# The block-diagonal keys of layer 2: four scaled copies on ACT in place of one instruction on DVE

## The reference

```python
HD, GROUPS = 8, 4
q = hidden_state @ Wq + bq
k = encoder_hidden_state @ Wk + bk
v = encoder_hidden_state @ Wv + bv
q = q.reshape(b, l, KVH, GROUPS, HD).transpose(0, 2, 3, 1, 4)
k = k.reshape(b, s, KVH, HD).transpose(0, 2, 1, 3)
v = v.reshape(b, s, KVH, HD).transpose(0, 2, 1, 3)
scores = jnp.einsum('bkgld,bksd->bkgls', q, k) / sqrt(HD) + encoder_attention_mask
attn = jax.nn.softmax(scores, axis=-1)
out = jnp.einsum('bkgls,bksd->bkgld', attn, v) ... @ Wo + bo
x = out + hidden_state          # then layer norm with gamma and beta
```

## Time and profile before

| what | value |
|---|---|
| median of 3 runs | 1674.97 us (1672.3 to 1674.98) |
| the profiled execution: its own time, its span | 1674.09 us, 1672.4 us |
| mean granted TensorE clock | 0.969 |
| busy share of the span: PE, PEld, DVE, ACT, POOL | 92%, 79%, 66%, 40%, 27% |
| layer 2, from its first instruction to its last | 1188.9 to 1354.9 us of the span |

### The profile page before, as it was taken

One profiled execution on the slowest core, in us unless ns is written; L12 is line 12 of the kernel. 1 busy time (PEld: TensorE's weight loads), 2 busy tenths in 40 slices (PEclk: granted clock), 3 DMA queues, 4 the chain that ended last, 5 costly groups with the idle time before them and its releaser, 6 DMA issues. The chain is left out here.

```text
span 1672.4 us, 33255 instructions
## 1 busy us (share of the span) xinstructions
PE 1545.5 (92%) x13291; PEld 1321.8 (79%) x13291; DVE 1103.6 (66%) x2377; ACT 672.5 (40%) x1270; POOL 454.6 (27%) x533
## 2 busy tenths in 40 slices
PE   4988999999999999999999999799788869999797
PEld 2656888888888888888888888789667748887697
DVE  6886666666666776667666666555499945776443
ACT  4654433343433434333333334332366634454221
POOL 2004020020110221200201110232288866562110
PEclk9998999999999999999999999999899979999899
DMA  4000010010000000000100000000410000000001
GB/s 131 1 0 26 14 39 14 1 39 14 27 13 14 26 14 14 26 14 13 39 14 9 31 26 11 20 20 0 84 56 1 2 1 2 3 2 2 1 1 50
DMA packets 44466, 34.12 MB, mean 20 GB/s; under 512 B 10658, under 2 KB 41384, under 8 KB 44200
## 3 DMA queue, kind: packets, MB, share of 16 engines
q1 hardware_dynamic: 44328, 32.17, 6.7%
HBM read 30.00 MB, written 2.10 MB: 19 GB/s over the span
## 5 line engine op out<-in xcount | busy, mean ns | idle before, releaser
L964 DVE STREAM_TRANSPOSE att_pt<-att_prob 32x256 f32<-32x256 f32 x496 | 215.7, 435 | 6.4
L864 ACT ACTIVATE split_q_sb<-psum,g_cols 128x512 f32<-128x512 f32 x128 | 88.3, 690 | 321.7 <-PE psum L732 321.7
L781 PE MATMUL psum<-att_wo_hi,att_ot_hi 128*128 128x256 f32 x512 | 149.2, 291 | 2.5 <-DVE att_ot_lo L977 1.4
L935 DVE TENSOR_REDUCE att_rmax<-psum 128x6 f32<-128x390 f32 (+1 forms) x96 | 49.2, 513 | 151.3 <-PE psum L694 151.3
L781 PE MATMUL psum<-att_wo_lo,att_ot_hi 128*128 128x256 f32 x512 | 144.6, 282 | 0.0
L781 PE MATMUL psum<-att_wo_hi,att_ot_lo 128*128 128x256 f32 x512 | 144.6, 282 | 0.0
L764 PE MATMUL psum<-att_pt,att_v_sb 128*128 128x128 f32 x1024 | 128.6, 279 | 3.5 <-DVE att_ot_lo L977 3.5
L987 DVE TENSOR_TENSOR g_x_res<-psum,g_x_res 128x256 f32<-128x256 f32 x128 | 54.3, 424 | 114.7 <-PE psum L781 88.3
L764 PEld LDWEIGHTS psum<-att_pt,att_v_sb 128*128 128x128 f32 x1024 | 122.9, 193 | 7.9 <-DVE att_ot_lo L977 3.7
L867 ACT ACTIVATE att_k_sb<-psum,g_cols 128x512 f32<-128x512 f32 x128 | 88.1, 688 | 80.9 <-PE psum L732 80.9
L732 PE MATMUL psum<-split_feat_hi,split_wide_hi 128*128 128x512 f32 x256 | 103.7, 405 | 4.5 <-DVE split_feat_lo L1011 3.3
(11 more groups left out here) (287 smaller groups left out, 3944.8 us busy)
## 6 DMA issues: line engine op xcount, KB each, us to landing
g_ctx_f<-in_L_xattn_wq SPq DMA_DIRECT2D x32, 128.0 KB, 2.2
g_ctx_f<-in_L_xattn_wk SPq DMA_DIRECT2D x32, 128.0 KB, 2.3
g_ctx_f<-in_L_xattn_wv SPq DMA_DIRECT2D x8, 512.0 KB, 3.8
g_ctx_f<-in_L_xattn_wo SPq DMA_DIRECT2D x8, 512.0 KB, 3.8
c_ctx_tok<-in_ctx SPq DMA_DIRECT2D x4, 512.0 KB, 5.6
g_x_res<-in_x SPq DMA_DIRECT2D x4, 512.0 KB, 8.7
g_w<-in_L_xattn_mlp_w SPq DMA_DIRECT2D x2, 1024.0 KB
out<-g_x_res SPq DMA_DIRECT2D x1, 2048.0 KB, 7.5
```

The costliest lines, as they stand in the source:

```text
L781: mm = pe.matmul(o_ps[p % 2], a, b, start=(h == 0 and t == 0), stop=(not last and h == HG - 1 and t == 2))
L864: act.activation(q_sb[:, h, :], q_ps[:, :], ACT.Identity, bias=G.cols[:, layer, head:head + 1]).then_inc(q_ready, 1)
L935: dve.tensor_reduce(rmax[:, a:b], s_ps[group][:, :, :], X_AXIS, ALU.max).then_inc(max_done, 1)
L964: turned = dve.transpose(pt[to:to + 32, :, :, r, u, 32 * a:32 * a + 32].rearrange("p h a t -> p (h a) t"), by_pair[of:of + 32, :, u, 32 * ...
```

## The change

Three things are edited, all in `phase_grouped_attention`. `place_keys` is taken out of DVE's list, and `move_projected` on ACT gets four more activations between the queries and the values. Each writes one `k_bd[:, v, :]` (128x128) as Identity(scale * k_ps + bias), with a column of `spread` as scale and a column of the new tile `k_bias` as bias; the last one raises `k_done`. `k_bias` is made once, before the loop, by a DVE instruction on 128x4 that multiplies `spread` with the key bias, and ACT waits for it once. Last, `project(p)` on PE, which overwrites the PSUM bank, now waits for `v_done` in place of `k_done`, since the values are now the last that is read from the bank.

```diff
--- before.py
+++ after.py
@@ -1779,7 +1779,7 @@
         wq, wk = m.sb("wq", [P, KT, D]), m.sb("wk", [P, KT, P])
         cols, bv_wide, one = m.sb("cols", [P, 4]), m.sb("bv_wide", [P, P]), m.sb("one", [1, P])
         mask = m.sb("mask", [P, B, T])
-        folded, spread = m.sb("folded", [P, ROWS]), m.sb("spread", [P, 4])
+        folded, spread, k_bias = m.sb("folded", [P, ROWS]), m.sb("spread", [P, 4]), m.sb("k_bias", [P, 4])
         q_sb, k_bd = m.sb("q_sb", [P, 2, 2, 2, T]), m.sb("k_bd", [P, 2, 4, P])
         v_bd = m.sb("v_bd", [P, 4, 2, 2, 2 * ROWS])
         soft = m.sb("soft", [P, 2, TILES, 4, 2, T])
@@ -1793,6 +1793,7 @@
         c_ps, o_ps = c_bank[:, 0:D].rearrange("p (b c t) -> p b c t", b=2, c=2), c_bank[:, 0:D]
         cols_ps, bias_ps = p_bank[:, 0:4], c_bank[:, 0:D]
 
+        k_bias_done = m.sem("k_bias_done")
         mask_in, arrived, v_zero, folded_made, spread_made, one_made = (m.sem(n) for n in
             ("mask_in", "arrived", "v_zero", "folded_made", "spread_made", "one_made"))
         w_ready, cols_psum, cols_done, bv_done, bias_psum, bias_done = (m.sem(n) for n in
@@ -1859,7 +1860,7 @@
                 def project(p):
                     x_new, ctx = (t[:, :, p * P:(p + 1) * P] for t in (G.feat_f, G.ctx_f))
                     if p:
-                        pe.wait_ge(k_done, p)
+                        pe.wait_ge(v_done, p)
                     for c in range(2):
                         accumulate(q_ps[:, c, :], [(wq[:, k, c * P:(c + 1) * P], x_new[:, k, :]) for k in range(KT)])
                     accumulate(k_ps, [(wk[:, k, :], ctx[:, k, :]) for k in range(KT)])
@@ -1949,6 +1950,9 @@
                         a = act.activation(q_sb[:, p % 2, :, c, :], q_ps[:, c, :].rearrange("p (b t) -> p b t", b=2),
                                            ACT.Identity, bias=cols[:, c:c + 1])
                     a.then_inc(q_done, 1)
+                    for v in range(4):
+                        a = act.activation(k_bd[:, p % 2, v, :], k_ps, ACT.Identity, bias=k_bias[:, v:v + 1], scale=spread[:, v:v + 1])
+                    a.then_inc(k_done, 1)
                     for b in range(2):
                         for u in range(2):
                             a = act.activation(
@@ -1963,6 +1967,7 @@
                     act.activation(ot[:, :, :].rearrange("p c (b t) -> p b c t", b=2), c_ps, ACT.Copy).then_inc(ot_done, 1)
 
                 act.wait_ge(cols_done, 1)
+                act.wait_ge(k_bias_done, 1)
                 act.wait_ge(v_zero, 1)
                 for t in range(PAIRS + 3):
                     if there(t - 2):
@@ -2004,14 +2009,6 @@
                         dve.wait_ge(prob_ready, 4 * (p - 1) + 2 * half + 2)
                     dve.reciprocal(rinv[:, half, :], rsum[:, half, :]).then_inc(inv_done, 1)
 
-                def place_keys(p):
-                    dve.wait_ge(q_done, p + 1)
-                    dve.wait_ge(v_done, p + 1)
-                    if p >= 2:
-                        dve.wait_ge(s_psum, p - 1)
-                    dve.scalar_tensor_tensor(k_bd[:, p % 2, :, :], k_ps.unsqueeze(1).to_broadcast([P, 4, P]), cols[:, 2:3],
-                                             spread[:, :].unsqueeze(2).to_broadcast([P, 4, P]), ALU.add, ALU.mult).then_inc(k_done, 1)
-
                 def add_output(p):
                     dve.wait_ge(o_psum, p + 1)
                     dve.tensor_tensor(dst[:, p, :], o_ps, dst[:, p, :], ALU.add).then_inc(x_done, 1)
@@ -2029,6 +2026,7 @@
                 dve.wait_ge(cols_done, 1)
                 dve.tensor_copy(bv_wide[:, :], cols[:, 3:4].to_broadcast([P, P])).then_inc(bv_done, 1)
                 dve.wait_ge(spread_made, 1)
+                dve.tensor_scalar(k_bias[:, :], spread[:, :], cols[:, 2:3], None, ALU.mult).then_inc(k_bias_done, 1)
                 dve.wait_ge(bias_psum, 1)
                 dve.tensor_tensor(w.o_bias[:, :], w.o_bias[:, :], bias_ps, ALU.add).then_inc(bias_done, 1)
                 dve.wait_ge(mask_in, 32)
@@ -2039,8 +2037,6 @@
                         invert(t - 2, 1)
                     if there(t - 1):
                         add_mask(t - 1, 1)
-                    if there(t):
-                        place_keys(t)
                     if there(t - 1):
                         invert(t - 1, 0)
                     if there(t - 3):
```

## The result

The changed kernel takes 1681.58 us (median of 9 runs, 1679.3 to 1689.93), the kernel before 1674.62 (9 runs, 1672.3 to 1674.98). The ratio is 1.0057, 95% interval 1.004 to 1.0075: the change makes the kernel slower, by some 7 to 12.5 us. Five of the changed kernel's nine runs took 1679.3 to 1681.6, the other four 1684.8 to 1689.9, so its median lies nearer to the kernel before than its mean does. The profiled execution took 1681.35 us with a span of 1679.5.

A forecast was written before the change was run, and what follows sets the result against it. Loop A, 8.75 us a period, was taken as the bound, not DVE; Loop B at 9.01 replaces it. 10 x 0.26 + 3 x 1.23 + 1.3 = 7.6 us more gave 1682.1 us, range 1676.5 to 1689.

The forecast's parts named there:

- Loop A: Chain from DVE's mask step through POOL's subtraction and normalization, PE's second turn and scores to the next mask step: 8.75 us.
- DVE's relief: One DVE instruction of 0.74 us a pair removed, some 0.66 of DVE's sequence; claimed worth 0 in the loop.
- The first rival: DVE is the bound after all: each period loses 0.66 us, total 1667; chance 0.05.
- Loop B: Chain from scores through ACT's queries, values and `ot` to PE's outputs, bias product and second turn: 7.58 us, 9.01 after.
- The room of 1.17: What Loop B's 7.58 us lacked of Loop A's 8.75: all the room ACT's chain has in a period.
- The period, 9.01: Full-clock period after the change: Loop B's 7.58 us plus 1.43 for four ACT copies, +0.26 a period.
- With the clock down 10.62: Period that meets the low clock: Loop B's 9.19 us plus 1.43, against 9.39 before, +1.23.
- The start, +1.3: First pairs: keys ready 0.13 us sooner at pair 0, four copies delay pair 1's exponent by 1.43; net +1.3.
- Three periods with the clock down: Three of the 13 periods from pair 2 to pair 15 meet the low clock, each +1.23 us.
- The third rival: The clock falls in every second period, 7 times and not 3: +14.0 us, 1688 to 1689; chance 0.13.
- The hidden case: Copies cost 0.26 us each, or the clock no longer falls: +2.8 to +3.0, no measurable change; chance 0.22.
- +3.0 us: Low bound, copies adding 1.04 us: full-clock periods cost nothing, low-clock periods +2.1, start +0.9; 1677.1 to 1678.0.

The follow-up runs named there:

- the first experiment: Kernel before, with DVE making the keys only for pairs 0 and 1 and nothing added on ACT: 1674.00 us, ratio 1.0007.

## Why the prediction was right

- *Loop A sets the period, and DVE's relief is worth 0.* Shown by the first experiment: 8.75 with DVE idle 0.84. The first rival, DVE as the bound, is refuted where it was posed; DVE binds only once loop A is opened, at 8.49.
- *Loop B replaces A because `ot` is late.* Shown three ways: the period is 8.97 with ACT's load alone, 8.75 with the keys behind `ot`, and 8.75 with half the copies. The room of 1.17 lies where the runs put it: 0.7 and 1.00 fit, 1.37 does not.
- *The period, 9.01.* Measured 8.97. The copies take 0.469 each, but add 1.37 and not 1.43 ahead of the values.
- *With the clock down 10.62.* Measured 10.46 to 10.67, though with the low stretch in another place. I put the low stretch on scores and projection, as before. In the changed kernel it falls on the turn and the scores.
- *The start, +1.3.* Measured 1.2 up to the mask step of pair 1, in all traces of the two kernels within 0.1.
- *Three periods with the clock down.* Here the working was wrong. Of the thirteen periods before, two and not three met the low clock (9.39 and 9.42); the third low stretch that I counted lies in the period ahead of them (9.32). And I held the number fixed, where the changed kernel has four in two traces and three in one. Layer 2 grew by 10.3 us in the first pair of traces, not by 7.6: 1.2 at the start; 1.1 in the period before the thirteen (10.43 against 9.32), where I had put nothing; 7.9 in the thirteen; 0.1 at the end. Over all traces it is 167.3 against 157.1, so 10.2. The 1.1 can't be laid to the change: the same period is 10.02 in the second trace of the kernel before, and 10.51 with DVE relieved and nothing on ACT.
- *The total.* 1682.1 against 1681.58 looks closer than the working was. The profiled pair differs by 10.3 in layer 2 and by 7.1 in the span, because the rest happened to be 3.6 shorter; in the other two traces of the changed kernel it was not, and the ratio's middle, 1.0057, is 9.5 us. The direction and the rough size stand; the agreement within 1 us is luck, since the sum had too little low clock in layer 2, and the profiled run made up for part of it with a remainder 3.6 shorter.

The Trainium skill (Perfetto Trace Analysis, Optimizing Scalar/DVE Operations) says that offloading a saturated DVE may make sense. It gave nothing here in the order that the engines had: DVE's idle time grew and no period got shorter. With PE's order changed as well the period fell from 8.49 to 8.10, though the whole time does not show it clear of noise. What made the difference is whether a loop through other engines is longer than the saturated engine's own sum.

The third rival, more clock drops, did not take over: four and not seven. But it was right in kind: two more long periods than before in two traces and one more in the third, at 1.6 us each. Why there are more is open. The hidden case did not come about in the changed kernel, but it is what half the copies show, and the copies without the bias too, at 0.25 each. For that price I had worked out +3.0 us; it measured 0.9979, some 3.5 us less than the kernel before, since the low clock that the +3.0 counts on met one of thirteen periods there at most, and the rest of the program met less of it as well.

## What to carry to other kernels

Follow the releasers from one instruction to its next occurrence before moving work: if they add up to the period without passing through the busy engine, its relief is worth nothing, even at 95% busy. On the engine that takes the work ask what stands behind the new place, and how much that chain lacks of the longest loop; here 1.17 us were free, and the same four copies one place later, behind `ot`, cost the period nothing. Where an operand becomes ready earlier, look for the instruction on another engine whose place in the order can now be changed, since that is where the gain is.

## What the runs showed of the hardware

- Of the ACT copy of 128x128 from PSUM, a per-partition bias beside the per-partition scale costs 88 ns of 469, and the next copy starts 0.34 after the last, or 0.25 without the bias. The Trainium skill (ScalarE: Activation LUTs, What ACT_TABLE_LOAD costs) states about 93 ns for each such operand, with which these runs agree.
- A product one row deep and products 32 rows deep that follow it in PE's list ran at the same time and saved 0.2 us: their starts are 0.02 apart, and from the bias product to what follows the scores it is 1.50 in place of 1.71.
- The granted clock fell to about 0.55 for some 3.7 us though in the thirteen periods PE's products stood idle for no more than 1.15 us at a stretch (1.10 before). With two copies all thirteen periods are 8.74 to 8.76, and in the kernel before, at the same period, two of them are long. What makes the difference is open: the traces show where it fell, and not what decides it.
- Identical code behind a changed stage took 313.9 to 319.8 us from one trace to the next, a spread of more than half of the effect under study. The 3.6 us between the two lengths that occur most, 313.9 and 317.5, go with two low-clock stretches that are there or not. A stage is better compared by its own length in several traces than by the program's time.
